# A recommendation tower: the last block's layer 2 turned round, and layer 3 done on VectorE

## The chip, the cores and the metric

The kernel runs on one core of a Trainium2 chip. The metric is the device time of one execution in microseconds (us); less is better. TensorE (PE) does matrix multiplications in two records each, a weight load (PEld) and a matmul; VectorE (DVE), ScalarE (ACT) and GpSimd (POOL) do the rest, and SyncE (SP) issues most DMAs. A page calls the DMA issues of an engine its queue (SPq). Every float32 matmul of this kernel appears as two matmul records and two weight loads; a transpose appears as one of each.

## The reference, cut to what matters

```python
e = jnp.stack([tbl_f[ids[:, f]] for f in range(32)], axis=1)     # 512 samples x 32 fields x 256
z = einsum('bnd,bmd->bnm', e, e)[:, iu, ju]                      # products of all field pairs, 496 per sample
h = jnp.concatenate([z, dense_ctx], axis=1)                      # 512 x (496 + 16)
h = jnp.maximum(h @ W_top1 + b_top1, 0.0)                        # layer 1: 512 x 512
h = jnp.maximum(h @ W_top2 + b_top2, 0.0)                        # layer 2: 512 x 256
y = h @ W_top3                                                   # layer 3: 512 x 1
```

The line of `e` is shortened from 32 written-out lookups. All is float32, and both biases are not zero.

## The kernel before, in words

The 512 samples are worked through in 16 batches of 32. Of the 32 embedding rows of a sample, those of 4 tables (8 in the second half) are found by one-hot matmuls (L565) in tables that are held in SBUF in turn; the others are fetched from HBM by indirect DMAs that GpSimd issues (L346), 104 in all, and transposed by TensorE (L584). For each sample `dots` multiplies its 32 rows with each other (L614), 8 samples after 8, and VectorE and ScalarE move the products into `pairs` (L394, L480). The order of all this is written out by hand as rounds, one for each batch, and every engine's program goes through the same rounds in its own order.

The tower itself (layers 1 to 3) runs on blocks of 128 samples, 4 blocks in all (NB = 4). For the first three blocks layer 1 (L621) has weights from `w1_sb` and 128 samples as moving columns; layer 2 (L674) gives two chunks of 128 outputs (N2 = 2) by 4 steps each (N1 = 4), with `w2_sb` as weights and the samples of `h1` as moving columns; its result has outputs on partitions and samples along the row. So layer 3 (L682) is two matmuls with one column of weights each, `w3_sb`, over the samples, into one partition; ScalarE's `keep_y` (L505) copies these 128 values into the one-partition row `y`.

The last block can't wait for its four batches together, so its layer 1 is done batch by batch. `flip(m)` (L648) has the 32 samples of batch m as weights and 128 columns of `w1_sb` moved, for 8 values of j and 4 quarters (32 matmuls, 64 records); `copy_flipped(m)` copies the result to `flipped` (batches 0 and 3 on ScalarE, L492; 1 and 2 on VectorE, L399); `turn(m)` (L658) transposes it back on TensorE; `relu_turned(m)` (L496) on ScalarE for batches 0, 1 and 3, and a line of VectorE's (L430) for batch 2, take the maximum with zero into `h1`. After the last products of batch 15 (`move(NM - 1)`), the order on TensorE is `flip(2)`, `flip(3)`, `layer3(2)` (block 2's layer 3), `turn(1)`, `turn(2)`, `turn(3)`, and then the last block's layer 2: 8 matmuls, and `layer3(3)`. ScalarE has, behind its last move, `copy_flipped(3)`, `keep_y(2)`, `relu_turned(1)`, `relu_turned(3)`, the bias and maximum of layer 2's chunk 0 (L501) and `keep_y(3)`; VectorE has `copy_flipped(2)`, the maximum of batch 2 and the bias and maximum of chunk 1 (L432). SyncE waits for the fourth `keep_y` and stores the 512 values of `y`, 2 KB from one partition, in one DMA (L329), and waits until it has landed.

Buffers `flipped` and `h2` lie in the same SBUF bytes as `one_hot`, which is last read by the look-ups in round 6 (the semaphore `chunk_used` then stands at 64).

Of the kernel before, what the change touches and what calls it, by code (L numbers as in the profile page):

```python
# [7 lines left out]
F32 = mybir.dt.float32  # L8
# [67 lines left out]
PRODUCTS_FREE = 5  # L76


def build_tower(nc, table, first_ids, ids, small_tables, small_ids, dense, w1, w2, b2, w3, out):
    D = table.shape[1]  # L80
    DC = D // P
    B = out.shape[1]
# [11 lines left out]
    with ExitStack() as ctx:  # L94
# [3 lines left out]
        def sem(name):  # L98
            return ctx.enter_context(nc.semaphore(name))
# [13 lines left out]
        small_sb = sb("small_sb", [KR, TABLES, CHUNKS, D])  # L113
        high = sb("high", [KR, TABLES, CHUNKS, D], F32R)

        with nc.sbuf_tensor("flipped", [P, BATCHES, P], F32) as flipped, nc.sbuf_tensor("h2", [P, N2, BLOCK], F32) as h2:
            pass
        one_hot = sb("one_hot", [KR, ONE_HOTS, B], F32R)
        kept = sb("kept", [P, DC, B, LOOKED_UP[1]])
# [20 lines left out]

        flip_ps = [bank[:, 0:P] for bank in (banks[0], banks[4], banks[0], banks[3])]
        turn_ps = [bank[:, P:2 * P] for bank in (banks[0], banks[4], banks[0], banks[3])]
        last_l2_ps = [bank[:, 0:BLOCK] for bank in (xt_ps[2], xt_ps[0])]
        last_l3_ps = xt_ps[1][0:1, 0:BLOCK]

        first_ids_in = sem("first_ids_in")
        ids_in = sem("ids_in")
# [34 lines left out]
        h2_ready = sem("h2_ready")  # L182
        l3_done = sem("l3_done")
        y_ready = sem("y_ready")
        stored = sem("stored")

        def half_of(n):
# [96 lines left out]
        @block.sync  # L284
        def _(sp):
            sp.dma_start(first_sb[:], first_ids).then_inc(first_ids_in, 16)

            def load_dense(b):
                sp.dma_start(pairs[0:dense.shape[0], b % 2, 0, :],
                             dense[:, b * BLOCK:(b + 1) * BLOCK]).then_inc(dense_in[b % 2], 16)  # L290

            for k in range(LOOKED_UP[1]):
                if k >= TABLE_IDS:

                    sp.wait_ge(one_hot_ready, (k - TABLE_IDS + 1) * CHUNKS)
                if k:
                    of = looked_up_for(k)
                    sp.dma_start(small_ids_sb[:, k % TABLE_IDS, of], small_ids[:, k, of].to_broadcast([KR, of.stop - of.start])
                                 ).then_inc(small_ids_in[k % TABLE_IDS], 16)
                for c in range(0, CHUNKS, 2):  # L300
                    if k >= TABLES:

                        sp.wait_ge(chunk_used, (k - TABLES) * CHUNKS + c + 2)
                    first = c
                    if k == 0 and c == 0:

                        sp.dma_start(small_sb[:, 0, 0, :], small_tables[0][:, 0, :]).then_inc(first_chunk_in, 16)
                        first = 1
                    sp.dma_start(small_sb[:, k % TABLES, first:c + 2, :],
                                 small_tables[k][:, first:c + 2, :]).then_inc(small_in[k % TABLES][c // 2], 16)  # L310
                    if k == 0 and c == 0:
                        sp.dma_start(ids_sb[:], ids).then_inc(ids_in, 16)
                if k == 1:
                    for to, source in ((b2_sb, b2), (w3_sb, w3)):
                        sp.dma_start(to[:], source).then_inc(biases_in, 16)
                    sp.wait_ge(no_pairs_zeroed, 1)
                    load_dense(0)
                    load_dense(1)
            for j in range(JJ):

                sp.wait_ge(transposed, EARLY + j)
                sp.dma_start(w1_sb[:, j, :], w1[:, j, :]).then_inc(w1_in, 16)
            sp.dma_start(w2_sb[:], w2).then_inc(w2_in, 16)
            for b in range(2, NB):

                sp.wait_ge(l1_done, N1 * (b - 1))
                load_dense(b)
            sp.wait_ge(y_ready, NB)
            sp.dma_start(out, y[:]).then_inc(stored, 16)  # L329
            sp.wait_ge(stored, 16)  # L330

        @block.gpsimd
        def _(pool):
# [17 lines left out]
        def _(dve):  # L351
# [57 lines left out]
            for r in range(ROUNDS):  # L409
                if r:  # L410
                    move(r - 1)
                for two in twos_in(r + 1):
                    prepare(two)
                for n in KEPT_IN.get(r, ()):
                    take_kept(n)
                for f in fills_in(r):
                    if f == NF - 2:
# [4 lines left out]
                        for k in range(N2):  # L422
# [5 lines left out]
            copy_flipped(2)  # L428
            dve.wait_ge(turned, 3)
            nc.vector.tensor_scalar(*turned_parts(2), 0.0, None, ALU.max).then_inc(last_h1_dve, 1)  # L430
            dve.wait_ge(l2_done, NB * N2)
            nc.vector.tensor_scalar(h2[:, N2 - 1, :], last_l2_ps[N2 - 1], b2_sb[:, N2 - 1:N2], 0.0,  # L432
                                    ALU.add, ALU.max).then_inc(h2_ready, 1)

        @block.scalar
        def _(act):
# [80 lines left out]
            for r in range(ROUNDS):  # L517
# [14 lines left out]
                for f in fills_in(r):  # L532
# [4 lines left out]
                        relu_turned(0)  # L537
                    take_xt(f)
            move(NM - 1)
            copy_flipped(3)  # L540
            keep_y(NB - 2, l3_ps)
            relu_turned(1)
            relu_turned(3)
            relu2(NB - 1, last_l2_ps, range(N2 - 1))
            keep_y(NB - 1, last_l3_ps)

        @block.tensor
        def _(pe):
# [183 lines left out]
                    fill(f)  # L732
            for half in (2 * NM - 2, 2 * NM - 1):
                dots(half)
            flip(2)
            flip(3)
            layer3(NB - 2, l3_ps)
            for m in range(1, BATCHES):
                turn(m)

            pe.wait_ge(last_h1_act, len(TURNED_BY_ACT))
            pe.wait_ge(last_h1_dve, BATCHES - len(TURNED_BY_ACT))
            for n in range(N2):
                for k in range(N1):
                    layer2(NB - 1, n, k, last_l2_ps)
            layer3(NB - 1, last_l3_ps)


# [66 lines left out]
```

## Time and profile before

| | us |
|---|---|
| median of 3 runs | 239.85 (235.57, 239.85, 242.84) |
| the profiled execution, own time | 235.87 |
| its span, first to last instruction | 234.1 |
| busy in the span: TensorE matmul / weight load | 178.3 (76%) / 149.6 (64%) |
| busy: VectorE / ScalarE / GpSimd | 95.4 (41%) / 77.6 (33%) / 102.9 (44%) |
| mean granted TensorE clock | 0.854 of full |

The profiled execution's own time has 1.8 us outside its span. The page cuts the span into 40 equal slices of 5.85 us, and a digit is a share of a slice in tenths. A matmul record's length is modelled and overlaps the next one, so the distance between the starts of two records (their pitch) tells more than the length of one.

### The profile page before, as it was taken

The numbers are of one execution on the slowest core, as the hardware profiler recorded it, in microseconds if no ns is written. First come the engines' busy times: TensorE is split into PE (matmuls) and PEld (weight loads), VectorE is DVE, ScalarE is ACT, GpSimd is POOL, SyncE is SP. The second block draws the span as 40 slices with busy tenths as digits, with TensorE's granted clock in tenths as the row PEclk, the third lists the DMA queues.
The fourth block names the chain that finished last, engine by engine and source line by source line (L and its number), as shares of the span: only waits on it lengthen the run. The fifth ranks groups of instructions, "written<-read, shape, count | busy, mean of one in ns | idle before, by whom it ended". The sixth has DMA issues, their size and how long they took to land.

```text
span 234.1 us, 6208 instructions
## 1 busy us (share of the span) xinstructions
PE 178.3 (76%) x2678; PEld 149.6 (64%) x2678; DVE 95.4 (41%) x311; ACT 77.6 (33%) x190; POOL 102.9 (44%) x110
## 2 busy tenths in 40 slices
PE   7999944221998978798888594493939599999985
PEld 7688821001687866686767492482829499899874
DVE  2797220000737816759354015041311409544331
ACT  3374420130674773424023041060402026334122
POOL 2777777774475676435273327345442400000000
PEclk9999995555799988799799977587697769999999
DMA  5899455332487875435331304213130300000000
GB/s 150 302 370 319 122 156 152 109 99 85 130 291 210 284 250 187 137 113 176 118 104 42 85 3 112 67 42 97 48 92 0 92 3 4 6 3 4 4 6 0
DMA packets 12869, 26.77 MB, mean 114 GB/s; under 512 B 2917, under 2 KB 3881, under 8 KB 12842
## 3 DMA queue, kind: packets, MB, share of 16 engines
q0 software_dynamic: 4992, 13.64, 19.6%
q1 hardware_dynamic: 7706, 12.47, 16.4%
q8 instruction: 21, 0.34, 0.6%
q10 hardware_dynamic: 144, 0.26, 0.5%
q14 instruction: 6, 0.05, 0.1%
HBM read 26.36 MB, written 0.00 MB: 113 GB/s over the span
## 4 chain that ended last, share of the span: by engine, by line
PE 71%; issue 22%; DMA 2%; ACT 2%; DVE 1%; SPq 1%
PE bank L565 22%; PE bank L614 16%; PE xt_ps L584 14%; PE bank L621 12%; PE bank L648 3%; PE bank L674 2%; DMA small_sb<-small_tables 2%; PE xt_ps L674 1%; DVE pairs L394 1%; ACT high L450 1%; PE bank L682 1%; ACT xt L463 0%; ACT h L496 0%; DVE xt L377 0%; PE xt_ps L682 0%
## 5 line engine op out<-in xcount | busy, mean ns | idle before, releaser
L346 POOL DMA_INDIRECT rows<-table,row_ids x104 | 102.2, 983 | 80.9 <-PE xt_ps L584 43.0
L614 PE MATMUL bank<-xt 128*32 128x32 f32 (+1 forms) x1664 | 41.8, 215 | 25.5 <-issue 24.6
L614 PEld LDWEIGHTS bank<-xt 128*32 128x32 f32 (+1 forms) x1664 | 32.5, 125 | 35.4 <-issue 31.5
L463 ACT COPY xt<-xt_ps 128x512 f32<-128x512 f32 (+1 forms) x43 | 22.3, 551 | 92.1 <-PE xt_ps L584 67.9
L584 PE MATMUL xt_ps<-ident,rows 128*128 128x128 f32 x208 | 34.5, 311 | 15.7 <-issue 15.5
L394 DVE COPY pairs<-bank 32x64 f32<-32x64 f32 (+1 forms) x184 | 39.6, 215 | 5.2 <-PE bank L614 2.9
L377 DVE COPY xt<-xt_ps 128x512 f32<-128x512 f32 (+1 forms) x14 | 9.2, 654 | 75.7 <-PE xt_ps L584 75.7
L584 PEld LDWEIGHTS xt_ps<-ident,rows 128*128 128x128 f32 x208 | 27.3, 160 | 18.7 <-issue 17.1
L366 DVE TENSOR_SCALAR one_hot<-small_ids_sb,first_sb 128x512 fp32r<-128x512 int32 (+1 forms) x64 | 24.7, 422 | 35.9 <-remote 33.7
L565 PE MATMUL bank<-one_hot,high 128*128 128x512 f32 (+1 forms) x128 | 33.9, 378 | 5.4 <-issue 3.4
L565 PE MATMUL bank<-one_hot,low 128*128 128x512 f32 (+1 forms) x128 | 30.5, 358 | 3.5 <-issue 3.5
L621 PE MATMUL bank<-pairs,w_sb 128*128 128x128 f32 x192 | 30.7, 318 | 0.5 <-issue 0.5
L565 PEld LDWEIGHTS bank<-one_hot,high 128*128 128x128 f32 x128 | 22.3, 206 | 12.2 <-issue 9.6
L621 PEld LDWEIGHTS bank<-pairs,w_sb 128*128 128x128 f32 x192 | 27.6, 226 | 2.4 <-issue 2.1
L565 PEld LDWEIGHTS bank<-one_hot,low 128*128 128x128 f32 x128 | 22.5, 204 | 7.6 <-issue 4.8
L371 DVE TENSOR_TENSOR low<-small_sb,high 128x512 fp32r<-128x512 f32 x32 | 22.1, 690 | 1.6 <-ACT high L450 1.6
L458 ACT COPY kept<-bank 128x512 f32<-128x512 f32 (+1 forms) x16 | 13.1, 932 | 22.8 <-PE bank L565 14.8
L450 ACT CAST high<-small_sb 128x512 fp32r<-128x512 f32 x31 | 18.6, 630 | 5.7 <-DMA small_sb<-small_tables 3.9
L480 ACT COPY pairs<-bank 32x56 f32<-32x56 f32 (+1 forms) x72 | 14.8, 205 | 4.9 <-PE bank L614 3.9
L648 PE MATMUL bank<-w_sb,pairs 128*32 128x128 f32 x256 | 8.2, 274 | 1.0 <-issue 0.9
L648 PEld LDWEIGHTS bank<-w_sb,pairs 128*32 128x32 f32 x256 | 6.9, 110 | 1.8 <-issue 1.3
L488 ACT ACTIVATE h<-bank 128x512 f32<-128x512 f32 x3 | 1.8, 599 | 15.0 <-PE bank L621 15.0
(36 smaller groups left out, 45.6 us busy)
## 6 DMA issues: line engine op xcount, KB each, us to landing
small_sb<-small_tables SPq DMA_DIRECT2D x31, 256.0 KB
w_sb<-w SPq DMA_DIRECT2D x8, 256.0 KB
rows<-table,row_ids POOLq DMA_INDIRECT x104
small_ids_sb<-small_ids SPq DMA_DIRECT2D x3, 256.0 KB
small_ids_sb<-small_ids SPq DMA_DIRECT2D x4, 128.0 KB
w_sb<-w SPq DMA_DIRECT2D x1, 512.0 KB
small_ids_sb<-small_ids ACTq DMA_DIRECT2D x1, 256.0 KB
small_sb<-small_tables SPq DMA_DIRECT2D x2, 128.0 KB, 3.5
```

Of the source, the lines that this page charges most:

```text
L346: nc.gpsimd.indirect_dma_start(rows[:, i % ROWS, :], None, table, bass.IndirectOffsetOnAxis(ap=row_ids[:, i:i + 1], axis=0)).then_inc(gath ...
L366: nc.vector.tensor_scalar(one_hot[:, i % ONE_HOTS, of], small_ids_sb[:, k % TABLE_IDS, of], chunk_rows_sb[:, c:c + 1], None, ALU.is_equal) ...
L371: nc.vector.tensor_tensor(low[:, k, c - 1:c + 1, :], small_sb[:, k, c - 1:c + 1, :], high[:, k, c - 1:c + 1, :], ALU.subtract).then_inc(lo ...
L394: done = nc.vector.tensor_copy(to, source)
L450: nc.scalar.copy(high[:, k, c:c + 2, :], small_sb[:, k, c:c + 2, :]).then_inc(high_ready, 1)
L463: nc.scalar.copy(*fill_parts(f)).then_inc(xt_act, 1)
L480: done = nc.scalar.copy(to, source)
L565: last = nc.tensor.matmul(banks[FOUND_BANKS[k][d]][:, of], part[:, k % TABLES, c, d * P:(d + 1) * P], one_hot[:, i % ONE_HOTS, of], start= ...
L584: last = nc.tensor.transpose(xt_ps[f % 3][:, at:at + P], rows[:, i % ROWS, c * P:(c + 1) * P], ident[:])
L614: done = nc.tensor.matmul(dots_ps[later(n)][n % 2][quads, g, :], x, x, start=(c == 0), stop=(c == DC - 1))
L621: done = nc.tensor.matmul(to, w1_sb[:, j, n * P:(n + 1) * P], pairs[:, b % 2, j, :], start=(j == 0), stop=(j == JJ - 1))
L648: done = nc.tensor.matmul(flip_ps[m][Q * q:Q * (q + 1), :], pairs[:, b % 2, j, m * SAMPLES:(m + 1) * SAMPLES], w1_sb[:, j, q * P:(q + 1) * ...
```

## The change

For the last block alone, layer 2 has the samples of `h1` as weights and the 256 columns of `w2_sb` moved: 4 matmuls in place of 8, each with 256 columns in place of 128, into one bank whose partitions are the samples. Since the bias now runs along the row, it is added by a fifth matmul, with a 128 x 128 tile of ones as weights and `b2_rows` moved (row 0 is the bias, the other 127 rows are zero); it stands on TensorE behind `flip(3)` and ahead of `layer3(2)`. VectorE takes the maximum with zero, multiplies with `w3_rows` (layer 3's weights in every partition) and sums along the row in one operation, into `last_y`, one value in each of 128 partitions. ScalarE's and VectorE's bias and maximum of the last block, `layer3(3)` and `keep_y(3)` are gone.

The store is split in two: the first 384 values from `y` as before, and the last 128 from `last_y`, 4 bytes from each of 128 partitions. SyncE loads `b2_rows` and `w3_rows` (128 KB each) behind its last load of `dense`; VectorE sets the ones in round 7. `turn(1)` moves ahead of `flip(2)` on TensorE, and `relu_turned(1)` ahead of `copy_flipped(3)` and `keep_y(2)` on ScalarE. All new buffers lie over `one_hot`, as `flipped` does.

```diff
--- before.py
+++ after.py
@@ -76,7 +76,7 @@
 PRODUCTS_FREE = 5
 
 
-def build_tower(nc, table, first_ids, ids, small_tables, small_ids, dense, w1, w2, b2, w3, out):
+def build_tower(nc, table, first_ids, ids, small_tables, small_ids, dense, w1, w2, b2, w3, b2_rows_in, w3_row, out):
     D = table.shape[1]
     DC = D // P
     B = out.shape[1]
@@ -113,7 +113,11 @@
         small_sb = sb("small_sb", [KR, TABLES, CHUNKS, D])
         high = sb("high", [KR, TABLES, CHUNKS, D], F32R)
 
-        with nc.sbuf_tensor("flipped", [P, BATCHES, P], F32) as flipped, nc.sbuf_tensor("h2", [P, N2, BLOCK], F32) as h2:
+
+        with (nc.sbuf_tensor("flipped", [P, BATCHES, P], F32) as flipped, nc.sbuf_tensor("h2", [P, N2, BLOCK], F32) as h2,
+              nc.sbuf_tensor("ones", [P, P], F32) as ones, nc.sbuf_tensor("b2_rows", [P, H2], F32) as b2_rows,
+              nc.sbuf_tensor("w3_rows", [P, H2], F32) as w3_rows, nc.sbuf_tensor("weighted", [P, H2], F32) as weighted,
+              nc.sbuf_tensor("last_y", [P, 1], F32) as last_y):
             pass
         one_hot = sb("one_hot", [KR, ONE_HOTS, B], F32R)
         kept = sb("kept", [P, DC, B, LOOKED_UP[1]])
@@ -140,8 +144,7 @@
 
         flip_ps = [bank[:, 0:P] for bank in (banks[0], banks[4], banks[0], banks[3])]
         turn_ps = [bank[:, P:2 * P] for bank in (banks[0], banks[4], banks[0], banks[3])]
-        last_l2_ps = [bank[:, 0:BLOCK] for bank in (xt_ps[2], xt_ps[0])]
-        last_l3_ps = xt_ps[1][0:1, 0:BLOCK]
+        last_l2_ps = xt_ps[2][:, 0:H2]
 
         first_ids_in = sem("first_ids_in")
         ids_in = sem("ids_in")
@@ -182,6 +185,9 @@
         h2_ready = sem("h2_ready")
         l3_done = sem("l3_done")
         y_ready = sem("y_ready")
+        rows_in = sem("rows_in")
+        ones_set = sem("ones_set")
+        last_y_ready = sem("last_y_ready")
         stored = sem("stored")
 
         def half_of(n):
@@ -325,9 +331,16 @@
 
                 sp.wait_ge(l1_done, N1 * (b - 1))
                 load_dense(b)
-            sp.wait_ge(y_ready, NB)
-            sp.dma_start(out, y[:]).then_inc(stored, 16)
-            sp.wait_ge(stored, 16)
+
+            sp.wait_ge(chunk_used, 2 * TWOS)
+            sp.dma_start(b2_rows[:], b2_rows_in).then_inc(rows_in, 16)
+            sp.dma_start(w3_rows[:], w3_row.to_broadcast([P, H2])).then_inc(rows_in, 16)
+            first = B - BLOCK
+            sp.wait_ge(y_ready, NB - 1)
+            sp.dma_start(out[:, 0:first], y[:, 0:first]).then_inc(stored, 16)
+            sp.wait_ge(last_y_ready, 1)
+            sp.dma_start(out[:, first:].rearrange("a (p b) -> (a p) b", b=1), last_y[:]).then_inc(stored, 16)
+            sp.wait_ge(stored, 32)
 
         @block.gpsimd
         def _(pool):
@@ -409,6 +422,10 @@
             for r in range(ROUNDS):
                 if r:
                     move(r - 1)
+                if r == len(TWOS_IN):
+
+                    dve.wait_ge(chunk_used, 2 * TWOS)
+                    nc.vector.memset(ones[:], 1.0).then_inc(ones_set, 1)
                 for two in twos_in(r + 1):
                     prepare(two)
                 for n in KEPT_IN.get(r, ()):
@@ -428,9 +445,10 @@
             copy_flipped(2)
             dve.wait_ge(turned, 3)
             nc.vector.tensor_scalar(*turned_parts(2), 0.0, None, ALU.max).then_inc(last_h1_dve, 1)
-            dve.wait_ge(l2_done, NB * N2)
-            nc.vector.tensor_scalar(h2[:, N2 - 1, :], last_l2_ps[N2 - 1], b2_sb[:, N2 - 1:N2], 0.0,
-                                    ALU.add, ALU.max).then_inc(h2_ready, 1)
+            dve.wait_ge(rows_in, 32)
+            dve.wait_ge(l2_done, (NB - 1) * N2 + 1)
+            nc.vector.scalar_tensor_tensor(weighted[:], last_l2_ps, 0.0, w3_rows[:], ALU.max, ALU.mult,
+                                           accum_out=last_y[:]).then_inc(last_y_ready, 1)
 
         @block.scalar
         def _(act):
@@ -537,12 +555,10 @@
                         relu_turned(0)
                     take_xt(f)
             move(NM - 1)
+            relu_turned(1)
             copy_flipped(3)
             keep_y(NB - 2, l3_ps)
-            relu_turned(1)
             relu_turned(3)
-            relu2(NB - 1, last_l2_ps, range(N2 - 1))
-            keep_y(NB - 1, last_l3_ps)
 
         @block.tensor
         def _(pe):
@@ -732,18 +748,22 @@
                     fill(f)
             for half in (2 * NM - 2, 2 * NM - 1):
                 dots(half)
+            turn(1)
             flip(2)
             flip(3)
+
+            pe.wait_ge(ones_set, 1)
+            pe.wait_ge(rows_in, 32)
+            nc.tensor.matmul(last_l2_ps, ones[:], b2_rows[:], start=True, stop=False)
             layer3(NB - 2, l3_ps)
-            for m in range(1, BATCHES):
+            for m in range(2, BATCHES):
                 turn(m)
 
             pe.wait_ge(last_h1_act, len(TURNED_BY_ACT))
             pe.wait_ge(last_h1_dve, BATCHES - len(TURNED_BY_ACT))
-            for n in range(N2):
-                for k in range(N1):
-                    layer2(NB - 1, n, k, last_l2_ps)
-            layer3(NB - 1, last_l3_ps)
+            for k in range(N1):
+                done = nc.tensor.matmul(last_l2_ps, h1[:, (NB - 1) % 2, k, :], w2_sb[:, k, :], start=False, stop=(k == N1 - 1))
+            done.then_inc(l2_done, 1)
 
 
 def kernel(**inputs):
@@ -804,6 +824,8 @@
         "w2": a["W_top2"].reshape(H1 // P, P, -1).transpose(1, 0, 2),
         "b2": a["b_top2"].reshape(-1, P).T,
         "w3": a["W_top3"].reshape(-1, P).T,
+        "b2_rows_in": np.pad(a["b_top2"][None], ((0, P - 1), (0, 0))),
+        "w3_row": a["W_top3"].reshape(1, -1),
     }
     arrays = {k: np.ascontiguousarray(v) for k, v in arrays.items()}
     nc = bacc.Bacc("TRN2", target_bir_lowering=False, num_devices=1)
```

## Rows read from the trace of the kernel before

**Rows 1.** The page: head, and slices of 5.85 us with the granted TensorE clock.

```profile
span 234.1 us, 6208 instructions
...
PEclk9999995555799988799799977587697769999999
```

**Rows 2.** The chain of work that ended last, from 224.5 us on (start us, us, what).

```profile
224.53 0.23 DVE pairs L394
224.77 0.04 issue
224.81 0.41 PE bank L648 x3
225.22 0.89 issue
226.10 1.83 PE bank L648 x59
...
228.10 0.27 ACT flipped L492
228.36 0.20 ACT y L505
...
228.57 0.51 ACT h L496 x2
229.07 0.04 issue
229.12 2.07 PE xt_ps L674 x16
...
231.21 0.36 DVE h L432
231.57 0.04 issue
231.61 0.61 PE xt_ps L682 x4
...
232.25 0.26 ACT y L505
```

**Rows 3.** Timeline of all engines, 222 us to the end.

```profile
224.81 0.14 PEld L648 LDWEIGHTS bank<-w_sb,pairs 128*32 128x32 f32 x3 [0.34 <-DVE pairs L394]
...
227.78 0.49 PE L682 MATMUL bank<-h,w_sb 128*1 128x128 f32 x3
...
228.21 0.55 PE L658 MATMUL bank<-ident,flipped 128*128 128x128 f32 x3
...
232.53 0.24 SPq L329 DMA_DIRECT2D out<-y  x1
```

**Rows 4.** Groups of instructions by line and form, whole span, VectorE's widths.

```profile
L371 DVE TENSOR_TENSOR low<-small_sb,high 128x512 fp32r<-128x512 f32 x32 | 22.1, 690 | 1.6 <-ACT high L450 1.6
...
L377 DVE COPY xt<-xt_ps 128x512 f32<-128x512 f32 x12 | 8.3, 692 | 69.6 <-PE xt_ps L584 69.6
...
L377 DVE COPY xt<-xt_ps 128x256 f32<-128x256 f32 x2 | 0.9, 426 | 6.1 <-PE xt_ps L584 6.1
...
L399 DVE COPY flipped<-bank 128x128 f32<-128x128 f32 x2 | 0.6, 291 | 1.3 <-PE bank L648 1.2
```

**Rows 5.** SyncE's waits: waited for, us in total, times, longest.

```profile
SPq L94 <- DMA out<-y: 0.9, 1, 0.9
```

**Rows 6.** DMA issues of the whole span: KB each, us from issue to landing.

```profile
small_sb<-small_tables SPq DMA_DIRECT2D x2, 128.0 KB, 3.5
...
first_sb<-first_ids SPq DMA_DIRECT2D x1, 8.0 KB, 3.8
```

**Rows 7.** DMA from 195 to 198 us, in 40 slices of 0.075 us.

```profile
GB/s 0 0 0 0 0 0 0 0 0 0 0 0 0 0 0 0 7 218 0 7 20 27 20 20 14 0 0 0 0 0 0 0 0 0 0 0 0 0 0 0
```

**Rows 8.** VectorE's timeline from 134 to 160 us.

```profile
140.78 2.73 DVE L394 COPY pairs<-bank 32x56 f32<-32x56 f32 x12
143.53 0.43 DVE L385 COPY xt<-kept 128x512 f32<-128x512 f32 x1
155.34 0.69 DVE L377 COPY xt<-xt_ps 128x512 f32<-128x512 f32 x1 [11.38 <-PE xt_ps L584]
```

**Rows 9.** Table by stage: busy time, granted clock, DMA share.

```profile
192.00:222.00 30.00, 29.44 (x848) 26.98 (x847) 16.22 (x65) 12.80 (x41) 0.00 (x0) 1.00 0.02 5
```

## The prediction

> **What bounds the kernel now.** I read three views in this order. First the page's head and its row of slices [rows 1]: the reader is to see that the clock granted to TensorE falls in several slices up to about 190 us and is full in the last seven. Then the table by stage [rows 9]: from 192 to 222 us TensorE's matmuls are busy 29.44 of 30 us at the full clock. Up to there TensorE sets the time, and the change touches nothing of its work there. Last the chain of waits from 224.5 us on [rows 2], because everything that the change removes lies in it: VectorE's last copy of products ends at 224.77; TensorE does `flip(3)`, with a hole of 0.89 us that no wait explains; ScalarE then has `copy_flipped(3)`, `keep_y(2)` and two maxima, to 229.07; layer 2 runs from 229.12 to 231.2; VectorE takes 0.36, layer 3 0.61, `keep_y(3)` 0.26 us; the store is issued at 232.53 [rows 3]. In these 8 us no two engines overlap for long, so a microsecond saved there is one microsecond of the time, and one added as well. The sum below is made against the profiled execution, 235.87 us with a span of 234.1. The median of the three runs is 239.85, 4.0 above it, so I carry the difference over to the median.
>
> **Part 1: up to the last block's layer 2.** `turn(1)` ahead of `flip(2)` is one transpose of some 0.11 us (three lie in the 0.55 us from 228.21, the last one's 0.3 included [rows 3]). TensorE's weight loads stood idle for 0.34 us ahead of `flip(3)`, waiting for VectorE's move [rows 3]; that hides it. If it hid nothing, it would cost 0.2. On ScalarE `relu_turned(1)` then falls in the idle time behind the move, and one of the two maxima goes from the chain, half of 0.51 us, 0.25 [rows 2].
>
> Against that stands the bias matmul, which is in TensorE's order between `flip(3)` and `layer3(2)`, with `layer3(2)`, `turn(2)` and `turn(3)` queued behind it. It has two records of 256 columns. The price of a column: layer 3's four records of 128 columns with one column of weights take 0.61 us [rows 2], the last one being about 0.27 long, so 0.11 us of pitch each; layer 2's sixteen with 128 columns of weights take 2.07, so 0.12 each. The moving columns set the pitch, not the weights. 256 columns are thus 0.22 us, and the bias matmul 0.44. It also needs the whole array, where layer 3's first record in the profile ran beside the last ones of `flip(3)` (three of four lie in the 0.49 us from 227.78 [rows 3]), so up to 0.2 more. Less the transpose that went ahead (0.11), `turn(3)` ends at 228.76 + 0.33 to 0.53, so 229.1 to 229.3; the last maximum (0.28) is queued behind `keep_y(2)`, which is itself done by then, and ends at 229.4 to 229.6 where it was 229.07. I take +0.35. Bounds: +0.6, and -0.25 if the bias matmul were wholly hidden.
>
> **Part 2: layer 2 turned round.** Eight records at 0.22 in place of sixteen at 0.11 to 0.12: the last starts 7 x 0.22 = 1.54 us after the first and lasts some 0.38 (0.27 for 128 columns and 0.11 for the other 128), with 0.1 of start-up as before, 2.0 against 2.07. I take -0.05; bounds -0.15 and +0.1. Half as many instructions do the same columns, and columns are what costs.
>
> **Part 3: behind layer 2.** What goes is 0.36 + 0.04 + 0.61 + 0.02 + 0.26 = 1.29 us from layer 2's end to the store's issue [rows 2]. What comes is one VectorE operation on 128 x 256 from PSUM. Copies from PSUM take 692 ns for 512 columns and 426 for 256, 1.04 ns a column, and 291 for 128; a two-operand operation on 512 takes 690, no more [rows 4]. The removed one with bias and maximum had 0.36 for 128; with 128 columns more it is 0.49. The trace shows no operation with a sum beside its result. Its price lies between nothing and a further small operation, 0.29 by the copy of 128 columns; I take 0.1, as it moves one value. So 0.59 in place of 1.29, -0.70; bounds -0.86 (the plain copy's 0.43) and -0.50. The Trainium skill, "VectorE: DVE Perf Modes", section "Two Vector instructions with no wait between them", says that an operation which also writes out its accumulator is two instructions, the main one and a read. No row shows one; by that rule the saving would stand nearer to 0.5 than to 0.86.
>
> **Part 4: the store.** Now 2 KB leave one partition; the issue takes 0.24 us [rows 3] and SyncE waits 0.9 for the landing [rows 5], 1.15 together. After the change the last store has 128 pieces of 4 bytes, and the span ends with it. Two rows bound the price of many pieces. `dense` brings 17 rows of 512 B in a quiet stretch, in six slices at about 20 GB/s [rows 7]: 512 B by 20 GB/s is 26 ns a row, one behind the other; 128 of these make 3.3 us. `first_sb`, 128 rows of 64 B, landed 3.8 us after its issue, 2.65 more than the store, but beside big loads at the very start, of which one of 128 KB needed 3.5 [rows 6]; so most of the 3.8 isn't the number of rows. The lower bound is nothing, if the pieces are spread over the 16 engines. I take +0.8, nearer to `first_sb`, whose 128 rows are this form, less what it shares with its neighbours. The first store, of 384 values, is issued about 3 us earlier, when SyncE has nothing else, and is hidden; should it be late, both land together.
>
> The Trainium skill, "DMA: Bandwidth & Descriptors", section "Specifications", says that transfers under 512 bytes make the DMA engine read, modify and write; it speaks against this store, and is weighed as the third case. Its section "Anatomy of one DMA — SWDGE (gpsimd) path" puts the fixed cost at about 2 us, mostly the write's confirmation, whatever the size; the trace's 1.15 us for issue and landing is less. By that section the store would cost nearly the same as before, and the sum below would be 0.8 lower.
>
> **Part 5: what is hidden.** The two loads of 128 KB wait for `chunk_used` (met long before) behind the last load of `dense`, issued at about 195.4 us; DMA is busy 2% from 192 to 222 us [rows 9], and they are needed at 228. If they came late, TensorE would stop at `rows_in` with everything of the tail behind it. VectorE's setting of the ones falls in round 7, between its move ending at 143.5 and a stretch of 11.38 us idle [rows 8]: about 0.3 us in front of `take_kept(9)`, covered by that. Its wait on `chunk_used` is met, since the products of batch 6, which it has just moved, come behind the last look-up in TensorE's order. Both cost nothing.
>
> **The sum.** +0.35 - 0.05 - 0.70 + 0.80 = +0.4 us: 236.3 for an execution like the profiled one, 240.2 against the median. The bounds together: -0.25 - 0.15 - 0.86 + 0 = -1.3 and 0.6 + 0.1 - 0.5 + 3.3 = +3.5. A measurement of this kernel tells about 2% (4.8 us) from no change.
>
> **The rivals.** *Gain (0.17).* The pieces are spread and the store costs nothing more, the bias matmul hides, and the hole of 0.89 us in `flip(3)` [rows 2], which nothing in the program asks for, isn't there after the change: -1.3 - 0.9 = -2.2, 233.7, or 237.6 against the median. For it: `flip(2)` shows no such hole. Against: the layout of the instructions up to `flip(3)` hardly changes.
>
> *Loss by the store (0.13).* The 128 writes of 4 bytes fall into one stretch of 512 bytes of `out` and go one by one at the pace of `dense`, 26 ns each: +3.3 - 0.4 = +2.9, 238.8, or 242.8. This is slower than before, and it decides from 0.4 / 128 = 3 ns a piece on; over 2% only from (4.8 + 0.4) / 128 = 41 ns, for which I give 0.03 of the 0.13. The skill's rule on less than 512 bytes points here.
>
> *The stretches at a lower clock fall otherwise (0.10).* The three runs before lie 7.3 us apart, and the clock falls in several slices [rows 1]. Work that the change doesn't touch thus moves the time by more than the whole edit, to either side: 235 or 244.
>
> *The change doesn't do what it says:* if the sum along the row were a pass of its own over 256 columns, VectorE would need 0.43 more and part 3 would give 0.27; +0.8 in all, inside the forecast's case.
>
> **How the numbers follow.** The forecast has 0.60, with a range of its own of 238.5 to 243.3. The range for 8 in 10 takes in the gain, the store's loss and most of the spread of runs: 235.5 to 243.8. Faster by over 2% comes from the clock's case alone, 0.07; slower by over 2% from it, 0.05, and from the store, 0.03; within 2% is 0.85.
>
> **What would show it.** In the changed profile: the bias matmul as two records about 0.22 apart behind `flip(3)`, and layer 2 starting 4.7 us or so behind VectorE's last copy where it was 4.35 (less 0.9 if the hole is gone); 8 records of layer 2 in about 2.0 us, under 1.5 if loads set the pitch after all; one VectorE operation of 0.5 to 0.6 us; then SyncE's wait for `out`, 1.7 us if part 4 holds, 0.9 if the pieces cost nothing, 4 if they go one by one. `rows_in` must be met long before 228 us. The prediction is wrong if this wait is over 6 us, if TensorE waits for a load, or if stretches before 190 us move by more than the tail.

## The result, and the profile after

The changed kernel took 246.1 us (median of 4 runs, 244.65 to 248.53), the kernel before 238.25 (median of 4 runs made alongside and earlier). The ratio is 1.038, with an interval of 1.031 to 1.046: slower by 7 to 11 us. The executions of a kernel fall into a faster and a slower group; ratios and their intervals are of the faster ones alone, medians are of all, so the two can differ a little. The forecast was 240.2, range 235.5 to 243.8. The profiled execution of the changed kernel has a time of 248.53 us and a span of 246.6.

The chain of waits of the changed kernel, from VectorE's last stretch on, answers to [rows 2]. It reaches only to 238.8 us, and the span ends at 246.6:

```profile
229.47 2.08 PE bank L664 x66
231.55 0.92 issue
232.47 1.95 PE bank L664 x62
234.41 0.63 PE xt_ps L757 x2
235.04 0.53 PE bank L698 x4
235.57 0.38 PE bank L674 x2
235.95 0.02 issue
235.97 0.29 ACT h L514
236.26 0.04 issue
236.31 2.01 PE xt_ps L765 x8
...
238.41 0.42 DVE weighted L450
```

L757 is the bias matmul, L698 `layer3(2)`, L674 the turns, L765 layer 2. The timeline of the changed kernel adds what follows:

```profile
229.25 1.81 DVE L407 COPY pairs<-bank 32x56 f32<-32x56 f32 x8 [1.43 <-PE bank L630]
...
234.97 0.60 PE L698 MATMUL bank<-h,w_sb 128*1 128x128 f32 x4
...
238.76 0.08 DVE L450 DVE_READ_ACCUMULATOR weighted<-xt_ps,w_rows 128x1 f32 x1
238.88 0.34 SPq L342 DMA_DIRECT2D out<-last_y  x1
```

SyncE's waits of the changed kernel answer to [rows 5]:

```profile
SPq L94 <- DMA out<-last_y: 7.0, 1, 7.0
```

Here is the loss: 7.0 us of waiting for the store where it was 0.9. The DMA table of the last stretch, 238 to 246.6 us in slices of 0.215 us, shows when the data were moved:

```profile
GB/s 0 0 0 0 0 0 0 0 3 0 0 0 0 0 0 0 0 0 0 0 0 0 0 0 0 0 0 0 0 0 0 0 0 0 0 0 0 0 0 0
DMA packets 144, 0.00 MB, mean 0 GB/s; under 512 B 144, under 2 KB 144, under 8 KB 144
```

All 144 packets (128 pieces and 16 more; the store of the kernel before shows 2 packets, one piece and one more) lie in the one slice from 239.7 to 239.9. The page gives their time as 0.9% of 16 engines' 8.6 us, some 1.2 us in all; so at least six engines shared them (an estimate: 1.2 us within 0.215). The DMA engines are done with the pieces after 0.2 us; 6.3 more microseconds pass until SyncE sees the store as landed (238.88 + 0.34 + 7.0 = 246.2). In the kernel before the last packet is done by 233.25 and the wait over at 233.7.

From VectorE's last copy (its end at 229.25 + 1.81 = 231.06) to the store's issue there are 7.82 us, before 7.76 (224.77 to 232.53); so the rest of the edit gains and loses the same. The profiled executions also differ by 6.3 us ahead of that point (231.06 against 224.77). Part of that can be chance: one execution is the slowest of its kernel's four runs (248.53) and the other, at 235.87, near the fastest of its own. Whether the change has a share in it is a suspicion that experiments 9 to 14 test.

### The profile page after: what moved, and what is told of

Its sections match the earlier page's. It is cut to its first block, busy times and chain, and to the rows that moved or that the text cites. A ratio compares the mean times of both kernels' runs of the same rounds, so it can differ in the third digit from the quotient of the medians.

```text
span 246.6 us, 6193 instructions
## 1 busy us (share of the span) xinstructions
PE 176.2 (71%) x2668; PEld 150.7 (61%) x2668; DVE 95.8 (39%) x313; ACT 76.9 (31%) x188; POOL 103.6 (42%) x110
## 4 chain that ended last, share of the span: by engine, by line
PE 71%; issue 21%; another core or an unknown queue 2%; ACT 2%; DVE 1%; POOL 0%; POOLq 0%; DVEq 0%
PE bank L581 21%; PE bank L630 16%; PE xt_ps L600 13%; PE bank L637 12%; PE bank L664 3%; PE bank L690 2%; PE xt_ps L717 2%; PE xt_ps L765 1%; ACT kept L476 1%; PE bank L698 1%; ACT xt L481 0%; PE bank L674 0%; DVE xt L390 0%; PE xt_ps L757 0%
## 5 line engine op out<-in xcount | busy, mean ns | idle before, releaser
L359 POOL DMA_INDIRECT rows<-table,row_ids x104 | 102.9, 990 | 87.4 <-PE xt_ps L600 50.4
L630 PE MATMUL bank<-xt 128*32 128x32 f32 (+1 forms) x1664 | 40.9, 215 | 27.6 <-issue 26.8
L600 PEld LDWEIGHTS xt_ps<-ident,rows 128*128 128x128 f32 x208 | 27.9, 164 | 20.7 <-issue 18.9
L581 PE MATMUL bank<-one_hot,high 128*128 128x512 f32 (+1 forms) x128 | 32.7, 373 | 9.8 <-DVE one_hot L379 7.1
L637 PE MATMUL bank<-pairs,w_sb 128*128 128x128 f32 x192 | 32.0, 327 | 1.2 <-issue 1.1
L581 PE MATMUL bank<-one_hot,low 128*128 128x512 f32 (+1 forms) x128 | 29.7, 352 | 3.7 <-issue 3.6
L637 PEld LDWEIGHTS bank<-pairs,w_sb 128*128 128x128 f32 x192 | 28.9, 234 | 2.5 <-issue 2.1
L398 DVE COPY xt<-kept 128x256 f32<-128x256 f32 (+1 forms) x8 | 2.8, 349 | 13.2 <-ACT kept L476 13.1
```

The costliest lines, as they stand in the source:

```text
L359: nc.gpsimd.indirect_dma_start(rows[:, i % ROWS, :], None, table, bass.IndirectOffsetOnAxis(ap=row_ids[:, i:i + 1], axis=0)).then_inc(gath ...
L581: last = nc.tensor.matmul(banks[FOUND_BANKS[k][d]][:, of], part[:, k % TABLES, c, d * P:(d + 1) * P], one_hot[:, i % ONE_HOTS, of], start= ...
L600: last = nc.tensor.transpose(xt_ps[f % 3][:, at:at + P], rows[:, i % ROWS, c * P:(c + 1) * P], ident[:])
L630: done = nc.tensor.matmul(dots_ps[later(n)][n % 2][quads, g, :], x, x, start=(c == 0), stop=(c == DC - 1))
L637: done = nc.tensor.matmul(to, w1_sb[:, j, n * P:(n + 1) * P], pairs[:, b % 2, j, :], start=(j == 0), stop=(j == JJ - 1))
```

## The experiments

Runs made together on one chip are called a session here. Each kernel is set against runs of the kernel before in its session; experiments 6 to 8 are one profiled execution each. Experiments 1 to 4 are one session, 5, 6 and 8 one, 7 and 9 to 11 one, and 12 to 14 one. The diffs are cut to what matters; `...` marks a cut.

**1. The changed kernel again.**

> The changed kernel itself, as the measure for the three beside it. Both theories expect 6 to 9 us more than before: 7.0 us of SyncE's wait for the landing of last_y again, and TensorE's hole of 0.9 us inside flip(3).

Measured: 245.6 us against 237.92, ratio 1.032 (1.026 to 1.038). SyncE waits 7.7 us for `last_y`.

**2. The changed kernel, last store from one partition.**

```diff
-            sp.dma_start(out[:, first:].rearrange("a (p b) -> (a p) b", b=1), last_y[:]).then_inc(stored, 16)
+            sp.dma_start(out[:, first:], y[:, 0:BLOCK]).then_inc(stored, 16)
```

> The changed kernel with one edit: once last_y is ready, the last 128 values of out are stored from one partition (512 bytes, block 0's values), so the last block's result is left out. Theory 1, the store's 128 pieces of 4 bytes are the whole loss: the wait falls from 7.0 to 0.9 us, the kernel gains 6 us against the changed one and is within 1 us of the kernel before. Theory 2, the loss is partly ahead of the tail (in the profile VectorE's last copy came 6.3 us later than before: the new loads, the ones set in round 7): it gains 6 us but stays 1.5 to 3 us above the kernel before. Theory 3, the wait is the fixed cost of a second store behind a first: it stays at 7 us.

Measured: 238.77 against 237.92, ratio 1.005 (1.001 to 1.009). SyncE's wait:

```profile
SPq L94 <- DMA out<-y: 0.8, 1, 0.8
```

The wait falls by 6.9 us and the time by 6.8. Theory 3 is out, since this kernel stores twice as well. What is left is 1.2 us by the ratio (0.3 to 2.2), between theories 1 and 2; experiment 14 takes it up.

**3. The kernel before, last store in 128 pieces.**

```diff
+            first = B - BLOCK
+            sp.wait_ge(y_ready, NB - 1)
+            sp.dma_start(out[:, 0:first], y[:, 0:first]).then_inc(stored, 16)
             sp.wait_ge(y_ready, NB)
-            sp.dma_start(out, y[:]).then_inc(stored, 16)
-            sp.wait_ge(stored, 16)
+            sp.dma_start(out[:, first:].rearrange("a (p b) -> (a p) b", b=1), h2[:, 1, 0:1]).then_inc(stored, 16)
+            sp.wait_ge(stored, 32)
```

> The kernel before with the split store alone: 384 values from y's row, and, once the last y is there, the last 128 values as 4 bytes from each of 128 partitions of h2, so the last block's result is left out. Theory 1: SyncE's last wait is 6.9 to 7.1 us in place of 0.9, the kernel 6 us slower than before and within 1.5 us of the changed one. Theory 2: as slow as theory 1 says, but 1.5 to 3 us faster than the changed kernel. Theory 3, that the price belongs to last_y being fresh from VectorE: 0.9 to 2 us of wait.

Measured: 244.47 against 237.92, ratio 1.022 (1.015 to 1.029). SyncE's wait:

```profile
SPq L94 <- DMA out<-h: 7.3, 1, 7.3
```

The form of the store alone, without any of the arithmetic, costs 6.6 us by the medians, 5.2 by the ratio (3.6 to 6.9), and 6.4 us of wait. `h2`'s values were 1.0 us old at the issue (written by 233.03, stored at 234.00) where `last_y` had just been written. That alone doesn't settle theory 3; experiment 6 does, where `w2_sb`, loaded long before, takes 6.7 us in the same form.

**4. The changed kernel, complete, with `last_y` turned into a row.**

```diff
+        last_l3_ps = xt_ps[1][0:1, 0:BLOCK]
...
-            sp.wait_ge(last_y_ready, 1)
-            sp.dma_start(out[:, first:].rearrange("a (p b) -> (a p) b", b=1), last_y[:]).then_inc(stored, 16)
+            sp.wait_ge(y_ready, NB)
+            sp.dma_start(out[:, first:], y[:, first:]).then_inc(stored, 16)
...
+            keep_y(NB - 1, last_l3_ps)
...
+            pe.wait_ge(last_y_ready, 1)
+            nc.tensor.matmul(last_l3_ps, last_y[:], ident[:], start=True, stop=True).then_inc(l3_done, 1)
```

> The changed kernel, complete, but last_y is turned into a row: one matmul with last_y as a single column of weights and the identity's 128 columns moved, keep_y into y on ScalarE, and one store of 512 bytes from one partition. By rows of before and after: VectorE 0.42 + 0.08, two records 0.38, ScalarE 0.26, hand-overs 0.1: 1.25 us behind layer 2 where the kernel before had 1.29. Theory 1: SyncE's wait 0.9 us, within 1 us of the kernel before, some 0.9 us above it by the later start of layer 2 (5.2 us behind VectorE's last copy in place of 4.35). Theory 2: 2 to 4 us above the kernel before.

Measured: 238.74 against 237.92, ratio 0.998 (0.993 to 1.002). The loss is gone. Its timeline has the new steps:

```profile
237.79 0.42 DVE L451 SCALAR_TENSOR_TENSOR weighted<-xt_ps,w_rows 128x256 f32<-128x256 f32 x1 [2.26 <-PE xt_ps L767]
...
238.28 0.38 PE L770 MATMUL xt_ps<-ident,last_y 128*1 128x128 f32 x2 [0.60 <-DVE weighted L451]
238.69 0.25 ACT L524 COPY y<-xt_ps 1x128 f32<-1x128 f32 x1 [3.07 <-PE xt_ps L770]
238.97 0.26 SPq L343 DMA_DIRECT2D out<-y  x1
```

1.2 us from VectorE's start to the issue, where the kernel before had 1.3 [rows 2]. To bring 128 values from 128 partitions into one costs 0.7 us by a matmul and a copy.

**5. The bias matmul moved ahead of the last products.** On top of experiment 4:

```diff
+            on_act, on_dve = moved_fills(NF - 3)
+            pe.wait_ge(xt_act, on_act)
+            pe.wait_ge(xt_dve, on_dve)
+            pe.wait_ge(ones_set, 1)
+            pe.wait_ge(rows_in, 32)
+            nc.tensor.matmul(last_l2_ps, ones[:], b2_rows[:], start=True, stop=False)
             for half in (2 * NM - 2, 2 * NM - 1):
                 dots(half)
```

It is gone from behind `flip(3)`, and `last_l2_ps` lies in `xt_ps[0]`.

> The changed kernel with last_y turned into a row by a matmul, and with the bias matmul moved ahead of the last batch's products, where TensorE waits 0.56 us for ScalarE's copy; it writes another bank for that. In four profiles layer 2 starts 3.96 us behind VectorE's last copy with the hole in flip(3) taken out, against 3.09 before. Theory: the bias matmul between flip(3) and layer3 is all of this, by waiting for the array to empty on both sides: 3.0 to 3.1 us, 0.9 less than without the move, and a total of 0 to 1 us below the kernel before. Rival: turn(1) ahead of flip(2) or the order on ScalarE costs it: it stays at 3.7 to 4.0.

Measured: 164.18 against 162.8, ratio 1.013 (1.006 to 1.021). The total was expected 0 to 1 us below the kernel before and is 2.2 above it (1.0 to 3.3); experiment 12 takes that up. Among these runs the kernel before took 162.8 us and not 238; the last section comes back to it. Its timeline:

```profile
157.08 2.08 PE L666 MATMUL bank<-w_sb,pairs 128*32 128x128 f32 x65 [0.69 <-issue]
...
158.95 0.60 PE L700 MATMUL bank<-h,w_sb 128*1 128x128 f32 x4
...
160.29 1.99 PE L770 MATMUL xt_ps<-w_sb,h 128*128 128x256 f32 x8 [0.37 <-ACT h L515]
```

The piece to compare is from the end of the hole in `flip(3)` to layer 2. Before it is 226.10 to 229.12, 3.02 us [rows 2]; in the changed kernel 232.47 to 236.31, 3.84; here 157.08 to 160.29, 3.21, a little over the 3.0 to 3.1 expected, and that includes the first two or three records of `flip(3)`, which the others have ahead of the hole. So the place of the bias matmul is the cause of at least 0.63 of the 0.82 us, and the rival (order of `turn(1)` or of ScalarE), by which the piece would have stayed at 3.7 to 4.0, is out. Layer 3's first record now starts at 158.95, before `flip(3)` has ended at 159.16, as in the kernel before; behind the bias matmul it started 0.55 us after that end (234.97 against 232.47 + 1.95).

**6. Stores by themselves.** Eleven DMAs behind the kernel before, to scratch tensors, each measured once:

```diff
             sp.wait_ge(stored, 16)
+            sp.dma_start(packed[:, 0:128].rearrange("a (p b) -> (a p) b", b=1), col).then_inc(probes[0], 16)
+            sp.wait_ge(probes[0], 16)
...
```

> The kernel before, and after its store eleven more DMAs on SyncE, each waited for before the next, to scratch tensors: their waits are the result, the total isn't. In order: 128 pieces of 4 bytes side by side (512 bytes); 32 such pieces; 64 such pieces; 128 pieces of 4 bytes 1024 bytes apart; 128 pieces of 4 bytes 64 bytes apart; 128 pieces of 512 bytes, 1024 apart; 16 pieces of 32 bytes side by side; 512 bytes from one partition; 128 pieces of 64 bytes side by side; 128 pieces of 4 bytes into SBUF, one in each partition; the fourth again. Theory A, small writes into the same stretch of HBM wait for each other: 7 us, 2.5, 4, then 1 to 1.5 for the spread ones, 1.2 for 512 bytes, 1 to 2 for 16 pieces, 0.9, and about 1 into SBUF. Theory B, every write below 512 bytes costs, wherever it goes in HBM: the spread pieces of 4 bytes and the pieces of 64 bytes need 7 us too, the 512-byte ones 1.2. Theory C, it is the number of pieces: all with 128 pieces need 7, those of 512 bytes and into SBUF too.

SyncE's waits (a wait stands at the line of the next instruction, so L341 is the first DMA of the list, L343 the second, L345 the third, and so on to L94 for the last):

```profile
SPq L341 <- DMA scratch<-w_sb: 6.7, 1, 6.7
SPq L345 <- DMA scratch<-w_sb: 6.1, 1, 6.1
SPq L343 <- DMA scratch<-w_sb: 2.8, 1, 2.8
SPq L351 <- DMA spread<-w_sb: 1.2, 1, 1.2
SPq L359 <- DMA h<-w_sb: 1.2, 1, 1.2
SPq L347 <- DMA spread<-w_sb: 1.1, 1, 1.1
SPq L357 <- DMA wide<-w_sb: 1.1, 1, 1.1
SPq L349 <- DMA spread<-w_sb: 1.1, 1, 1.1
SPq L94 <- DMA spread<-w_sb: 1.1, 1, 1.1
SPq L353 <- DMA scratch<-w_sb: 1.0, 1, 1.0
SPq L339 <- DMA out<-y: 0.9, 1, 0.9
SPq L355 <- DMA scratch<-w_sb: 0.8, 1, 0.8
```

128 pieces of 4 bytes side by side: 6.7 us. The same 128 pieces 1024 or 64 bytes apart: 1.1, and into 128 partitions of SBUF: 1.2 (L359). So it is neither the number of pieces (theory C) nor their being small (theory B; 128 pieces of 64 bytes also take 1.1). They have to be small and next to each other (theory A). The Trainium skill, "DMA: Bandwidth & Descriptors", section "Specifications", has transfers below 512 bytes read, modify and write; these rows show no price for being below 512 bytes as such.

**7. How near is too near.** Twelve more in the same manner, each measured once; the three forms that experiment 6 had as well (128, 64 and 32 pieces 4 bytes apart) come out within 0.4 us of their values there.

> The kernel before, and after its store twelve DMAs to scratch tensors of their own, each waited for before the next; their waits are the result. In order, pieces x bytes, distance of the starts in bytes: 64x4, 4; 128x4, 4; 128x4, 8; 128x4, 16; 128x4, 32; 16x4, 4; 64x8, 8; 32x16, 16; 128x8, 8; 128x16, 16; 128x32, 32; 32x4, 4. In the first probe 4-byte pieces 64 bytes apart were free, and pieces side by side took 6.7 (128), 6.1 (64) and 2.8 us (32). Theory A, pieces that share 64 bytes wait for each other: the wait above 1.1 us falls with the number of pieces in 64 bytes, 5.6 us at 16, 2 to 3 at 8, 1 to 1.5 at 4, under 1 at 2; 16 pieces of 4 bytes in one such stretch cost under 1 us. Rival, only the number of pieces in 512 bytes counts: 128 pieces 4 bytes apart like 128 in 512, 64x8 half of it, 32x16 a quarter, and 128x32 (16 in 512) 0.6 us above 1.1.

The waits stand at L346 for the first of the list, at L348 for the second, and on by two to L366 for the eleventh, L94 for the last:

```profile
SPq L348 <- DMA to<-w_sb: 6.7, 1, 6.7
SPq L346 <- DMA to<-w_sb: 6.5, 1, 6.5
SPq L358 <- DMA to<-w_sb: 3.0, 1, 3.0
SPq L94 <- DMA to<-w_sb: 2.7, 1, 2.7
SPq L350 <- DMA to<-w_sb: 2.4, 1, 2.4
SPq L362 <- DMA to<-w_sb: 2.3, 1, 2.3
SPq L354 <- DMA to<-w_sb: 1.2, 1, 1.2
SPq L352 <- DMA to<-w_sb: 1.1, 1, 1.1
SPq L364 <- DMA to<-w_sb: 1.1, 1, 1.1
SPq L366 <- DMA to<-w_sb: 1.1, 1, 1.1
SPq L360 <- DMA to<-w_sb: 1.0, 1, 1.0
SPq L356 <- DMA to<-w_sb: 1.0, 1, 1.0
```

| pieces x bytes | distance | wait, us |
|---|---|---|
| 128x4, 64x4, 32x4, 16x4 | 4 | 6.7, 6.5, 2.7, 1.0 |
| 128x4, 128x8, 64x8 | 8 | 2.4, 2.3, 3.0 |
| 128x4, 128x16, 32x16 | 16 | 1.1, 1.1, 1.0 |
| 128x4, 128x32 | 32 | 1.2, 1.1 |

The distance of the starts decides, not the size. The rival, the number of pieces in 512 bytes, is out: 128x4 at distance 8 has as many as 64x4 at distance 4 and takes 2.4 in place of 6.5. Theory A had the order right; but at a distance of 8 it expected 2 to 3 us above 1.1 and 128 pieces showed 1.2 to 1.3, and at a distance of 16 it expected a price that isn't there. Nor does it explain why 64 pieces side by side take as long as 128 and 16 cost nothing, or why 64 pieces at a distance of 8 took longer than 128 (3.0 against 2.3). These rows show when the price is paid; by what mechanism stays open.

**8. The hole in `flip(3)`.** `WARM_UP = 1` in place of 9.

> The kernel before with 1 warm-up matmul in place of 9, so TensorE has 32 instructions fewer ahead of everything else. Theory: the hole inside flip(3) is the arrival of a block of TensorE's instructions; it lies at a fixed place in the stream (after 3 weight loads of flip(3) before, after 2 or 3 in all the changed kernels), so here it comes 16 weight loads later, behind 18 to 20 of flip(3), and is a little shorter (0.6 to 1.0 us where it was 1.27). Rival, the hole belongs to the data (VectorE's and ScalarE's last copies into pairs): it stays behind 3 weight loads.

The chain of waits of this run:

```profile
153.46 0.84 PE bank L648 x19
154.31 0.55 issue
154.86 1.40 PE bank L648 x43
```

19 records of `flip(3)` in place of 3 [rows 2] stand ahead of the hole: 16 more, for the 32 instructions fewer at the very beginning, two to a record. In experiment 5, where the bias matmul's four records stand ahead of it as well, the hole comes right behind `flip(2)`, two records earlier than in the changed kernel. The hole has a fixed place in TensorE's stream of instructions and is none of the data's. That it is the arrival of a block of instructions fits this and is not shown further. It is in all profiles here, but from 0.2 us long (0.23 in experiment 2) to 0.9. Before and after the change it has nearly the same length (0.89 and 0.92), so it has no part in their difference; between other profiles it makes up to 0.7 us.

**9 to 11. The new loads.** First, in one session, the changed kernel again; the kernel before with the loads of `b2_rows` and `w3_rows` alone; and experiment 5 with the loads held until the last gathers have landed:

```diff
             sp.wait_ge(chunk_used, 2 * TWOS)
+            for i in range(NG - ROWS, NG):
+                sp.wait_ge(gathered[i % ROWS], 16 * (i // ROWS + 1))
             sp.dma_start(b2_rows[:], b2_rows_in).then_inc(rows_in, 16)
```

> The changed kernel once more, as the measure beside the next two. 6 to 9 us above before, whatever the level of the kernel before on this chip.

> The kernel before with the two new loads alone (128 KB each, behind SyncE's last load of dense; nothing reads them). The changed kernel with a one-piece store was 1.2 us (0.3 to 2.2) above before although its tail is as long (7.97 us against 7.99 behind VectorE's last copy, the hole left out), and with the matmul and the early bias 2.2 us (1.0 to 3.3). Theory 2a, the loads cost it, by holding up gathers: 1 to 2 us above before, most of all if the gathers still run when they are issued. Theory 2b, the loads are hidden and the rest is the first two changes' other work ahead of the tail or the scatter of the runs: within 0.5 us of before.

> The changed kernel with last_y turned into a row by a matmul, the bias matmul ahead of the last products, and the two loads held back until every gather has landed. Theory 2a: it loses the 1 to 2 us, and is 0 to 1 us faster than before. Theory 2b: it stays 1 to 2 us above before. Its tail is that of the version with the early bias, 7.9 us and the hole.

Measured, the kernel before at 163.95 us: changed kernel 168.67, ratio 1.033 (1.027 to 1.039); the loads alone 163.87, ratio 1.000 (0.992 to 1.007); late loads 163.21, ratio 0.996 (0.989 to 1.003). The loads alone cost nothing to within some 1.2 us, which speaks for 2b; the late loads fit both.

**12 to 14. Early and late loads side by side.**

> The version with the matmul for the row and the early bias, loads as in the changed kernel, beside its twin with late loads on one chip. It was 2.2 us (1.0 to 3.3) above before on a chip where the kernel before takes 163 us; the twin was 0.6 us below before (1.8 below to 0.5 above) on another. Theory 2a, the loads hold up gathers: 1 to 2.5 us above its twin. Theory 2b, the rest is scatter between sessions: within 0.8 us of its twin, both within 1 us of before.

> The twin with late loads. Theory 2a: at or up to 1 us below before, 1 to 2.5 us below the version with the loads in their first place. Theory 2b: within 0.8 us of it.

> The changed kernel with the last store from one partition (the last block's result left out), loads in their first place. 1.2 us (0.3 to 2.2) above before in the first session. Theory 2a: 1 to 2 us above before again. Theory 2b: within 0.8 us of before.

Measured, the kernel before at 238.3 us: early loads 239.66, ratio 1.001 (0.996 to 1.006); late loads 237.65, ratio 1.000 (0.996 to 1.003); the changed kernel with a one-piece store, as in experiment 2, 238.21, ratio 1.001 (0.997 to 1.005). None of the ratios differs from 1 by more than 0.1%, none of the intervals reaches beyond 0.6%. The medians of early and late loads, which are of all executions, do lie 2.0 us apart; by the ratios it is 0.3 us. So theory 2a isn't borne out: what the loads could cost and stay unseen is a little over 1 us. The 1.2 and 2.2 us of experiments 2 and 5 didn't come again; most likely they were scatter between sessions, for which their intervals were too narrow.

## Why the prediction was wrong

*Part 4, the store, is the step that failed.* It was taken at +0.8 with an upper bound of +3.3, and it is +6.2: issue and landing took 0.34 + 7.0 against 0.24 + 0.9. The prediction's own sign of being wrong, a wait of over 6 us, came. In experiments 2 to 4 the time goes with the form of this store and with nothing else of the edit. The two rows that bounded it, `first_sb` [rows 6] and `dense` [rows 7], are both reads from HBM, and the price lies in writes that fall next to each other in HBM. For the pieces as DMA traffic the lower bound was right (they are spread and gone in 0.2 us). What I didn't price is the time from the last packet to the landing: I took it as fixed, and it grew from some 0.4 us to over 6. The Trainium skill's "DMA: Bandwidth & Descriptors", section "Anatomy of one DMA — SWDGE (gpsimd) path", says of DMAs that GpSimd issues that the fixed part is mostly the confirmation of the write, whatever the size. The trace of this store, issued by SyncE, agrees in that 6.3 of the 7.0 us lie behind the last packet; it can't show that this is the confirmation, and constant it isn't.

*The rival "loss by the store"* named the place, and that it matters that the pieces fall into one stretch of 512 bytes. Its mechanism, pieces that go one by one at a fixed pace, with 26 ns a piece, isn't what the runs show: the packets are done in 0.2 us, and 64 pieces wait 6.1 to 6.5 us where 128 wait 6.7 and 16 wait 1.0. The measured 6.2 us over 128 pieces would be 48 ns, past its own threshold of 41 for a loss of over 2%. I gave that 0.03. With no row of a write in small pieces in the trace, the upper bound had no ground, and the case should have had more.

*Part 1* was +0.35, at most +0.6; it is +0.9: layer 2 starts 5.25 us behind VectorE's last copy (236.31 against 231.06) where it was 4.35, and 0.82 of that lies behind the hole, 3.84 against 3.02 us. The two records of the bias matmul start 0.32 us apart (234.34 and 234.66) where 0.22 was forecast, and layer 3's first record 0.31 behind the second. It starts 0.55 us behind the end of `flip(3)`; before it started 0.4 us ahead of that end (227.67 against 228.07). The 0.82 and the 0.11 of the transpose that went ahead make 0.9 us for a matmul that I took at 0.44 to 0.64. That the rest is the emptying of the array around a matmul that needs all of it fits these rows and isn't shown by them. The maximum that was to go from ScalarE's chain gave nothing: layer 2 starts 0.36 us behind the last transpose's end before and 0.37 after.

*Part 2* was -0.05: layer 2's records take 2.01 us against 2.07. Eight records of 256 columns cost what sixteen of 128 do.

*Part 3* was -0.70: from layer 2's end to the store's issue it is 0.56 us (238.32 to 238.88) against 1.34 (231.19 to 232.53), -0.78. The prediction's 1.29 for that piece leaves out two hand-overs of 0.05 us together. The operation took 0.42 and the read of its sum, a second instruction, 0.08, nearly all of it before the first had ended. The Trainium skill's "VectorE: DVE Perf Modes", section "Two Vector instructions with no wait between them", had said that there would be two; the trace agrees.

*Part 5* holds. The loads landed 3.2 and 4.6 us after their issue at 202 us, far ahead of the 234 where they are needed; by themselves they change nothing that shows (experiment 10, ratio 1.000).

*The sum.* With the measured parts it is +0.90 - 0.06 - 0.78 + 6.2 = +6.3 us, 2.6% of 238. The direct measurement is 7 to 11 us in the first session, and 6.1 to 9.0, then 4.5 to 6.4 in the next two, by their intervals. The 1 us or more by which the first lies above the sum is not explained; the later two enclose it. Without the store's form the change is worth nothing: the first three parts add up to +0.06, and experiments 2, 4 and 12 to 14 lie within about 0.5% of the kernel before. Even had part 4 cost nothing, the gain of part 3 would have gone into part 1.

*The hole* was handled as a chance that it might be gone. It stayed, 0.92 us, at nearly the same place of the stream. *The clock's case* had stretches ahead of the tail fall otherwise; in the profiled executions they did, by 6.3 us, as much as the tail. The mean granted clock was nearly the same (0.854 and 0.850); 3.6 of the 6.3 us are pauses of TensorE with no wait (48.3 and 51.9 us, see the last section), the rest the profiles leave open. That this isn't the change rests on experiments 10 and 12 to 14.

## What to carry to other kernels

128 values that lie one to a partition and are stored to adjacent 4-byte places in HBM cost 6 us until the store has landed, though the DMA engines are done after 0.2 us; bring them into one partition first (a matmul with the identity and a copy, 0.7 us here), or keep a layout that leaves them there. A removal at the end of a kernel has to be counted up to the landing of the last store, with a row of a write of that form, or else with an open upper end. And look at what stands beside a matmul that is put in: between `flip(3)` and `layer3(2)` this one cost 0.9 us where its columns are 0.44, and ahead of the last products, in a wait of 0.56 us, at most 0.2.

## What the runs showed of the hardware that wasn't expected

The wait for a store of many small pieces depends on their distance in HBM and hardly on their size: 128 pieces of 4 bytes take 6.7 us at a distance of 4 bytes, 2.4 at 8, 1.1 or 1.2 at 16 and more. It depends on their number too: at 4 bytes, 32 pieces take 2.7 and 16 take 1.0.

The kernel before took 238 us in three sessions and 163 in two others; on one and the same chip it took 162.8 in one and 238.3 in another. In the long ones TensorE stands with no wait to explain it, 39 to 53 us in all in each of the nine profiles; in the short ones it doesn't, but for the hole of `flip(3)`. The waits of TensorE in the first profile of the kernel before:

```profile
PE bank L614 <- issue: 24.6, 40, 1.2
PE xt_ps L584 <- issue: 15.5, 10, 3.1
PE bank L565 <- issue: 6.8, 11, 1.0
```

and those of the kernel before with the loads alone (experiment 10), in a short one:

```profile
PE xt_ps L590 <- DMA rows<-table,row_ids: 5.4, 4, 2.2
...
PE bank L620 <- ACT xt L469: 1.0, 2, 0.6
```

In `dots` (L614) the pauses are mostly of 0.4 to 0.5 us and nine times of 1.1 to 1.2, none after 192 us. These two profiles differ by 70.3 us in span (234.1 and 163.8). Of that 47.4 us are such pauses (48.3 against 0.9); another 26.8 are busy time of the same matmuls (178.3 against 151.5 us), at a mean granted clock of 0.85 of full against 0.98; for other engines TensorE waits 3.9 us less. What sets off the pauses, and whether the lower clock is their cause, their effect or neither, is open. They don't touch the question here: the wait for the store in 128 pieces was 7.0 to 7.7 us in the long ones and 6.9 in a short one, and every comparison of times is within a session.
